# A two-layer gated attention and feed-forward kernel: a first stage in another order, a finer end of attention, and normalised inputs turned by blocks through DRAM

## The reference, cut to what matters

```
x = x + tanh(g_xattn[0]) * linear_attention(layernorm(x), ctx)      # phase "A"
x = x + tanh(g_ffn[0])   * (gelu(layernorm(x) @ W1 + b1) @ W2 + b2) # phase "F"
x = x + tanh(g_xattn[1]) * softmax_readout(layernorm(x), ctx, mask) # phase "E", inputs called "L"
x = x + tanh(g_ffn[1])   * sum_g w[t,g] * (silu(x' @ G_g) * (x' @ U_g)) @ D_g   # phase "E", x' = layernorm(x), inputs called "M"
```

## Time and profile before

| | us |
|---|---|
| median of 3 runs (1902.69 to 1906.14) | 1904.37 |
| the profiled execution | 1901.83 |
| its span | 1900.0 |
| TensorE busy | 1847.5 (97%) |
| VectorE busy | 995.8 (52%) |
| ScalarE busy | 539.8 (28%) |
| GpSimd busy | 323.6 (17%) |

### The profile page before, as it was taken

How to read it: one execution, slowest core, us unless ns; L and a number is a source line. 1 busy time by engine, 2 the same in 40 slices (tenths; PEclk the granted TensorE clock), 3 DMA queues, 4 the chain that set the end, 5 groups by cost and what they waited for, 6 DMA issues and landing times.

```text
span 1900.0 us, 24571 instructions
## 1 busy us (share of the span) xinstructions
PE 1847.5 (97%) x9552; PEld 904.3 (48%) x9552; DVE 995.8 (52%) x2036; ACT 539.8 (28%) x801; POOL 323.6 (17%) x299
## 2 busy tenths in 40 slices
PE   6689999999999999999999999999999999999999
PEld 3355555544444444444444444444444444444444
DVE  4577776754545454554436554545545555545422
ACT  2233533411121222112112233333323333332321
POOL 1122332222020211202020011111111111111111
PEclk9899999999999999999999999999999999999999
DMA  3323443333224232332301200101010101000000
GB/s 110 91 62 106 133 148 97 100 107 77 79 61 133 60 101 89 78 105 53 89 23 40 67 9 1 54 1 53 1 53 1 53 1 54 1 23 1 1 23 22
DMA packets 135829, 112.09 MB, mean 59 GB/s; under 512 B 75554, under 2 KB 92066, under 8 KB 135714
## 3 DMA queue, kind: packets, MB, share of 16 engines
q1 hardware_dynamic: 135714, 110.53, 19.7%
HBM read 78.00 MB, written 32.51 MB: 58 GB/s over the span
## 4 chain that ended last, share of the span: by engine, by line
PE 83%; issue 9%; DVE 3%; POOL 2%; DMA 2%; ACT 1%; POOLq 0%; SPq 0%; DVEq 0%; ACTq 0%
PE bank L862 44%; PE bank L951 17%; PE bank L1031 10%; PE bank L931 4%; PE bank L871 3%; PE bank L897 2%; PE bank L916 1%; POOL arena L836 1%; PE bank L1018 1%; DVE arena L1217 1%; PE bank L966 1%; POOL arena L810 0%; PE bank L993 0%; DMA arena<-in_L_xattn_Wkv 0%; DMA arena<-x_after_ffn 0%
## 5 line engine op out<-in xcount | busy, mean ns | idle before, releaser
L862 PE MATMUL bank<-arena 128*128 128x512 f16 x4608 | 1044.5, 381 | 26.3 <-DVE arena L1284 11.2
L862 PEld LDWEIGHTS bank<-arena 128*128 128x128 f16 x4608 | 451.8, 98 | 558.8 <-issue 17.3
L951 PE MATMUL bank<-arena 128*128 128x512 f16 x1536 | 352.1, 379 | 1.3 <-DVE arena L1444 1.3
L1031 PE MATMUL bank<-arena 128*128 128x512 f16 x1152 | 264.3, 379 | 0.9 <-POOL arena L836 0.9
L1586 DVE SCALAR_TENSOR_TENSOR arena<-bank,arena 128x512 f32<-128x512 f32 x96 | 72.0, 750 | 329.0 <-PE bank L862 329.0
L1130 ACT ACTIVATE arena<-bank,arena 128x512 f32<-128x512 f32 x128 | 99.6, 778 | 489.0 <-PE bank L862 485.8
L951 PEld LDWEIGHTS bank<-arena 128*128 128x128 f16 x1536 | 150.1, 98 | 181.2 <-DVE arena L1444 1.8
L836 POOL TENSOR_TENSOR arena<-arena 128x512 f16<-128x512 f32 x96 | 111.0, 1157 | 625.9 <-ACT arena L1167 625.9
L1442 DVE TENSOR_SCALAR arena<-arena 128x512 f16<-128x512 f32 x128 | 65.7, 513 | 282.8 <-ACT arena L1130 282.5
L1031 PEld LDWEIGHTS bank<-arena 128*128 128x128 f16 x1152 | 112.0, 98 | 128.4 <-POOL arena L836 1.4
L1444 DVE SCALAR_TENSOR_TENSOR arena<-arena 128x512 f16<-128x512 f32 x128 | 118.0, 922 | 4.6
(11 more groups left out here) (159 smaller groups left out, 1213.0 us busy)
## 6 DMA issues: line engine op xcount, KB each, us to landing
arena<-in_L_ffn_proj SPq DMA_DIRECT2D x64, 256.0 KB, 2.9
arena<-in_L_ffn_gate_up_proj SPq DMA_DIRECT2D x96, 96.0 KB, 2.0
x_after_attention<-arena SPq DMA_DIRECT2D x8, 1024.0 KB, 5.2
arena<-x_after_attention SPq DMA_DIRECT2D x8, 1024.0 KB, 5.5
x_after_ffn<-arena SPq DMA_DIRECT2D x8, 1024.0 KB, 4.3
arena<-x_after_ffn SPq DMA_DIRECT2D x8, 1024.0 KB, 6.3
arena<-in_x SPq DMA_DIRECT2D x7, 1024.0 KB, 5.5
normalised_blocks<-arena SPq DMA_DIRECT2D x28, 256.0 KB, 2.0
```

The lines of the kernel that those rows point to most:

```text
L862: m = e.matmul(bank[b][:, :], wT[l][:, c, tile * P:(tile + 1) * P], y[h][:, c, :], start=n == 0, stop=n == NPASS - 1)
L951: m = e.matmul(bank[t][:, :], hv[h][:, 0, t * P:(t + 1) * P], w2T[l][:, j, :], start=j == 0 and i == 0, stop=j == NH - 1 and i == 2)
L1031: m = e.matmul(bank[t][:, :], hv[h][:, 0, t * P:(t + 1) * P], dnT[l][:, j, :], start=j == 0 and i == 0, stop=j == NR - 1 and i == 2)
```

## The change

1. First stage. Eight staging places for the first eight weight tiles (query and gate), so that all eight are loaded at the start; tile 8 and later use the first four places as before. The order of the plan: `keysk` is split into `kmin` and `kphi`; statistics, norms and `wmax` of the query tiles are placed between them; the splits of the query weights stand before the third value projection, the maxima of the gate tiles between the value projections, their scale and splits behind the first `q`. `consts` keeps only the halved gate bias; the tables, `all b1` stand behind `numden` in front of `ctxmax`. `vmax`/`all v` stand behind the first `gate`, `pow v` behind the third. All four `kvsum` stand behind the gates.
2. End of attention. In the loop for batch 7, `numden` of batch 7 stands behind the gates, `att` and `attlo` of batch 7 between the `out` steps of batch 6; behind the loop there are only the four `out` of batch 7. The waits of `att`/`attlo` on `out` are by tile.
3. L and M inputs by blocks through DRAM. The side tasks become finer (statistics in two, each tile one task, two `whole` tasks of two), with pauses of 2 (batch 0) or 3 tasks behind the read-back. `attention_tasks` has 35 tasks for batches 1 to 7 and 30 for batch 0, where it had 22. Phase E takes a side task at three points for each hidden tile instead of two: behind `ge`, behind `ue` and behind `dn`.

```diff
+def place(w):
+    return w if w < 2 * NC else w % 4
+def before_in_place(w):
+    return w - (2 * NC if w < 3 * NC else 4)
 def in_blocks(i):
     ph, b = i
-    return ph == "F" and b > 0
+    return ph in "LM" or (ph == "F" and b > 0)
...
+    def block_tasks(i):
+        def stats(ts):
+            for t in ts:
+                add("stat", i, t)
+            if NT - 1 in ts:
+                add("rs", i)
+        def tile(t):
+            add("norm", i, t)
+            add("block", i, t)
+            add("bstore", i, t)
+            if t == NT - 1:
+                add("bload", i)
+        def whole(cs):
+            for c in cs:
+                add("whole", i, c)
+        return ([lambda: stats((0, 1)), lambda: stats((2, 3))] + [lambda t=t: tile(t) for t in range(NT)]
+                + [None] * (2 if i in (("L", 0), ("M", 0)) else 3) + [lambda: whole((0, 1)), lambda: whole((2, 3)), None])
...
+    add("kvk", 3, banks=1)
+    seen()
+    add("kphi", 2)
+    seen()
+    norm()
+    add("kmin", 3)
+    seen()
+    norm()
+    add("kphi", 3)
+    seen()
+    add("kvv", 0, banks=1)
+    norm(2)
+    add("kvv", 1, banks=1)
+    add("keysv", 0)
+    add("pow", "q")
+    split("q")
+    norm(2)
+    flush()
+    add("kvv", 2, banks=1)
+    seen(2)
+    add("keysv", 1)
+    seen(2)
+    add("kvv", 3, banks=1)
+    add("keysv", 2)
     add("small")
     add("xload", "A", 1)
     for j in range(NC):
         add("q", 0, j, banks=1)
+        if j == 0:
+            add("keysv", 3)
+            add("pow", "g")
+            split("g")
+        flush()
     add("consts")
     for j in range(NC):
         add("gate", 0, j, banks=1)
+        norm()
         if j == 0:
+            add("vmax")
+            add("all", "v")
+        if j == 2:
             add("pow", "v")
         weights(N_O)
+    for t in range(4):
         add("kvsum", t, banks=4)
+        if t < 2:
+            norm()
     for t in range(NT):
+        norm()
         add("numden", 0, t, banks=2)
         weights(N_O)
+    add("tables")
+    add("all", "b1")
     add("ctxmax")
     add("all", "c")
...
+            if b == NB - 1 and j > 0:
+                add("numden", b, j - 1, banks=2)
...
+            else:
+                if t == 0:
+                    add("numden", b, NT - 1, banks=2)
+                add("att", b, t, banks=1)
+                if t > 0:
+                    add("attlo", b, t - 1)
...
+        pause = [None] * (1 if b == 0 else 2)
+        return [L[0], both(split, L[1]), *L[2:], lambda: add("scores", b, banks=1), *pause,
+                lambda: add("pturn", b, banks=1), lambda: add("read", b, banks=NT), *M,
+                lambda: add("router", b, banks=1), *pause, *pause, lambda: add("rturn", b, banks=1)]
```

More of the change, by code:

```diff
@@ L104, in weight_loads @@
     def weight_loads():
-        while load[0] < min(N_D, post[0] + 4):
+        while load[0] < N_D and (load[0] < 2 * NC or post[0] > max(before_in_place(load[0]), load[0] - 4 * NC)):
             add("wload", load[0])
@@ L169, in make_plan, with norm, seen, split @@
     norms = ln_tasks(("A", 0), apart=True)
[L170 to L173, removed]
+    def norm(k=1):
+        for _ in range(k):
             norms.pop(0)()
[L175 to L186, removed]
+    def seen(k=1):
+        for _ in range(k):
+            how, name, t = GROUPS[pre[0]]
+            add("wmax", pre[0])
+            pre[0] += 1
+            if t == NC - 1:
+                add("all", name)
+    def split(name):
+        for _ in range(NC):
+            add("wsplit", post[0])
+            late.append(lambda w=post[0]: add("wlo", w))
+            post[0] += 1
+        weight_loads()
+    add("kvk", 0, banks=1)
+    add("kmin", 0)
+    add("kvk", 1, banks=1)
+    norm()
+    add("kphi", 0)
+    norm()
+    add("kmin", 1)
+    add("kvk", 2, banks=1)
+    norm()
+    add("kphi", 1)
+    norm()
+    add("kmin", 2)
+    add("kvk", 3, banks=1)
[5 more added lines that the diff above has]
+    seen()
+    norm()
+    add("kphi", 3)
[14 more added lines that the diff above has]
+    add("keysv", 2)
     add("small")
@@ L190, in make_plan @@
         add("q", 0, j, banks=1)
[L191 to L194, removed]
+        if j == 0:
[3 more added lines that the diff above has]
+        flush()
+    scaled.update("qg")
     add("consts")
-    add("all", "b1")
-    add("vmax")
-    add("all", "v")
     add("xload", "A", 2)
@@ L257, in make_plan @@
             add("xload", "F", b + 2 - NB)
[L258 to L263, removed]
+    add("attlo", NB - 1, NT - 1)
+    for t in range(NT):
+        add("out", NB - 1, t, banks=1)
         some()
@@ L267, in make_plan @@
     weights_until(N_B)
[L269 to L286, removed]
     P_.ring, P_.turn = [4, 5, 6, 7], 0
@@ L348, in make_plan, with apart @@
     while side:
-        side.pop(0)()
+        f = side.pop(0)
+        if f:
+            f()
     add("xload", "E", 1)
     add("xload", "E", 2)
+    def apart():
+        f = side.pop(0) if side else None
+        if f:
+            f()
     total = NB * NR
@@ L426, in build @@
     attw = [at(176 + 2 * i, TOK).rearrange("p (j n) -> p j n", j=NC) for i in range(2)]
-    stg = [at(182 + 2 * i, D) for i in range(4)]
+    stg = [at(182 + 2 * i, D) for i in range(4)] + [at(52.5 + 2 * i, D) for i in range(4)]
     top = [190.0]
@@ L509, in build @@
     x_out = [sem(f"x_out{i}") for i in range(5)]
-    w_in = [sem(f"w_in{i}") for i in range(4)]
+    w_in = [sem(f"w_in{i}") for i in range(8)]
     last_out, craw_in, b2_in = sem("last_out"), sem("craw_in"), sem("b2_in")
@@ L636, in pieces @@
         return found
-    w_landed, landed = {}, [0] * 4
+    w_landed, landed = {}, [0] * 8
     for w in range(N_D):
-        landed[w % 4] += 16 * len(pieces(w))
-        w_landed[w] = landed[w % 4]
+        landed[place(w)] += 16 * len(pieces(w))
+        w_landed[w] = landed[place(w)]
     def y_ready(w, i):
```

68 lines of the change are left out of this document (32 added, 36 removed).

## The result

| | before | after |
|---|---|---|
| median | 1904.05 us (1901.76 to 1907.4, 19 runs) | 1910.52 us (1904.77 to 1918.08, 19 runs) |
| span of the profiled execution | 1900.0 | 1908.7 |
| TensorE busy | 1847.5 | 1828.7 |
| GpSimd busy | 323.6 | 395.1 |

The account below looks back on a forecast made before the run. TensorE, full from the fourth of 40 slices, was taken as the bound. Terms -9.5 - 5.1 - 2.4 = -17.0 us against the profiled 1901.83 gave 1884.8; that execution stood 2.5 us below the median, so forecast 1887.4 us, range 1867 to 1903.

Parts of the forecast that it names:

- Bound: Whole kernel: TensorE is full from the fourth of 40 slices; only less TensorE work or filled holes can win.
- part 1: First stage's new order: `q` of batch 1 14.1 us earlier, 4.6 given back; -9.5 us, bounds -14 and -4.
- Part 2: End of attention: the 3.15 us hole before `out` of batch 7 and its slow clock go; -5.1 us, bounds -5.1 and 0.
- Turns: Inputs of scores and router: 64 of TensorE's 132 turns go, 0.432 us each, -27.6 us.
- The router's chain: Second feed-forward: mix 10 waits on VectorE for the router's chain; TensorE waits 1.3 us at `dn` 10, seven times, +9.1 us.
- The passage: First to second feed-forward: holes ahead of `scores`, `router` and behind `router`, with slow clock; +16.1 us, bounds +8 and +22.
- Both are met or missed by 0.4 us; I add 1 us for all: Second feed-forward: low halves done at 17.3 to 19.1 and 22.6 to 24.4, `scores` reached at 18.8, `router` at 24.0; +1 us.
- Rival 3: Second feed-forward: read-back late in every batch, 14 us per us late, gain gone from 1.2; 1915 to 1929 us; chance 0.07.
- Rival 4: Second feed-forward and passage: VectorE and GpSimd block each other, low halves 1.6 us, +5 and +2 us; 1894 us; chance 0.12.

Follow-up runs that it names:

- the repaired kernel: Changed kernel with router and scores one place later, batch 0 turned by TensorE, and the first feed-forward's old task list; 1863.95 us, ratio to before 0.9794.

## Why the prediction was wrong

- **Bound, and part 1.** Right: `q` at 41.27 (41.9), VectorE waiting for `all v` until 68.6 (69) and for the inverse root until 77.2 (77), `q` of batch 1 at 93.36 (92.9), then 5.19 us at the turn (4.4) with slow matmuls behind it. The part alone measures -9.7 for -9.5. What came out otherwise is that the hole at `q` of batch 1 stayed, 3.65 instead of 3.58: the stage moved forward as a whole.
- **Part 2.** Right: no hole ahead of `out` of batch 7, 5.3 to 7.1 us for 5.1.
- **Turns.** Right: the batches of the repaired kernel show 0.436 us for each (0.432 in the sum).
- **The router's chain.** Right: forecast 1.3 us, seven times, at `dn` 10 for GpSimd's low half; measured 1.17 us, six times (7.9 us in 7, of which the last, 0.9, was there before). In the one case left (`router` at 1480.96) the matmuls behind the `router` ran slow, and TensorE came late enough not to wait. The sum was read a little high: 1272.32 - 1264.53 - 0.75 is 7.0 and not 7.1 us, so the chain is 10.3 and the wait 1.1 us. Its cause is shown by the router's later place.
- **The passage.** Right: 4.2, 2.5 and 6.0 us forecast, and the clock behind them; in the time line:

```profile
1023.85 2.72 PE L1036 MATMUL bank<-arena 128*128 128x64 f16 x48 [4.33 <-issue]
1026.38 3.86 PE L1021 MATMUL bank<-arena 128*128 128x512 f16 x12
...
1070.25 1.35 PE L1063 MATMUL bank<-arena 128*128 128x32 f16 x48 [1.80 <-issue]
1077.64 0.58 PE L1072 MATMUL bank<-arena 128*128 128x128 f16 x4 [6.04 <-DVE arena L1640]
1078.03 7.92 PE L932 MATMUL bank<-arena 128*128 128x512 f16 x24
```

12.2 us of holes, and 1.2 + 1.1 + 2.6 us over the 1.56, 2.75 and 5.34 us that the same groups take elsewhere: 17.1 for 16.1. Inside it two terms were off and cancel: the hole at the `router` is 1.8 and not 2.5 us, the clock 4.9 and not 3.4.
- **The step that failed** is "Both are met or missed by 0.4 us; I add 1 us for all", for the arrivals of L and M in the second feed-forward. They were missed by 0.2 to 2.9 us: 10.2 + 6.1 + 0.8 = 17.1 us of holes in 14 misses. Batch 2 shows the terms:

```profile
1204.07 0.71 DVE L1315 STREAM_TRANSPOSE arena<-arena 128x512 f32<-128x512 f32 x1
...
1207.68 4.66 SPq L797 DMA_DIRECT2D arena<-normalised_blocks  x4
...
1215.44 1.15 ACT L1145 ACTIVATE arena<-arena 128x512 f16<-128x512 f32 x2 [3.57 <-DMA arena<-normalised_blocks]
...
1216.14 5.40 POOL L893 TENSOR_TENSOR arena<-arena 128x512 f16<-128x512 f32 x4 [3.04 <-ACT arena L1145]
...
1221.65 1.56 PE L1036 MATMUL bank<-arena 128*128 128x64 f16 x48 [1.42 <-issue]
```

`ue` 2 ends at 1201.5, and TensorE reached `scores` at 1220.23, 18.7 us behind it (18.8 in the sum). The data was late by small amounts at each step. The last block ends 3.3 us behind `ue` 2, where the sum has 12.0 - 9.8 = 2.2. From there to the upper halves it is 10.7 us, where I took 9.8 and gave 10.5 as the bound; 2.9 of them pass before the read-back starts (2.07 taken; in the fourteen inputs 2.1 to 2.9). The four low halves take 5.4 us, 1.35 each, inside their bounds, and the last ends at 1221.54: 20.0 us behind `ue` 2, where the sum has 17.3 to 19.1. The first of these delays had no term at all: VectorE's copy waits for the store two tiles earlier, 0.54 us here and 2.09 in batch 3.

Even without that term the bounds did not allow 1 us "for all". With the arrival at its upper bound, 0.7 us later, the low halves would have missed `scores` by 1.0 and `router` by 1.1 us, some 15 us in fourteen. Rival 3 was this mechanism, with its slope of 14 us for each us and the gain gone at 1.2 us; the mean miss is 17.1 / 14 = 1.2 us. I gave it 0.07 and left its time out of the range.

- **The clock behind the misses.** Two of them were followed by slow matmuls, after holes of 2.89 and 1.61 us; about 2.9 us together, forecast 0:

```profile
1326.38 2.72 PE L1036 MATMUL bank<-arena 128*128 128x64 f16 x48 [2.89 <-issue]
...
1482.37 4.01 PE L1101 MATMUL bank<-arena 128*128 128x512 f16 x10
```

- **A second step that failed** is that the shorter task list brings no wait of its own: the stop in the first feed-forward costs 3.4 us and 1.6 of clock. The list was costed at nothing because its own instructions are the same; that it shifts the weights' steps among them wasn't looked at.
- **Rival 4** (VectorE and GpSimd hindering each other) is not needed: in the repaired kernel GpSimd's low halves take as long as in the changed one (1.25 us in the mean from 1100 to 1800 us in both, where its subtracts for `dn` take 1.16), far from the 1.6 us of the rival.

Between the two profiled executions lie +8.7 us (spans 1908.7 and 1900.0) where -17 was forecast: 25.7 us to find. The arrivals give 17.1 - 1 = 16.1, their clock 2.9, the stop 5.0, the passage +1.0, the router's chain 7.0 for 9.1, that is -2.1: 22.9 in all. The rest is small change behind each hole. From `rturn` to `rturn` TensorE's time less its waits is 100.23 us in the four batches without slow matmuls, each with three holes, where the repaired kernel takes 99.74, and 99.90 in those batches of the kernel with the later router that have a hole ahead of `scores` alone: half a microsecond in each of seven batches, 3.4 us. What it consists of is not shown.

## What to carry to other kernels

When work leaves the busiest engine for a path with a round trip, reckon for each consumer by how much the data beats its use, and multiply what is missing by how often it comes: a margin of 0.4 us in a loop passed 14 times is not a small term but, here, the largest error, and its bounds belong into the range with that factor. A consumer one place later in a written order costs nothing as long as what follows it has room, so place it by the late end of the arrival, not by its middle. And a task list that is made shorter moves everything that is filled in beside it: look at what those steps wait for.

## What was not expected of the hardware

The low clock doesn't go by the hole's length alone: matmuls were slow behind holes of 2.89, 3.37 and 4.33 us, and also behind one of 1.61 us (the group at 1482.37 above, after `router`'s wait at 1480.96), while that of 1.80 us at 1070.25 was followed by nothing slow at once, nor was one of 2.00 us ahead of `scores` of batch 7 (1743.80). Four DMAs of 256 KB each in 128-byte pieces take SP 4.66 us to issue, in rows of 8 KB 1.72 us, and yet in batch 2 the first upper half starts only 1.0 us sooner, and the last low half ends 1.6 to 2.1 us sooner in the mean. And a change of kind on GpSimd costs nothing where GpSimd has been idle long enough before it (24.48 us in the kernel with the old task list).
